# Second-layer attention by two passes: row maxima first, transposed exponentials after

## What is computed

```python
q = rope(x @ wq); k = rope(x @ wk); v = x @ wv       # 16 heads of 16; 4 key/value groups, each used by 4 heads
scores = einsum('bhqd,bhkd->bhqk', q, repeat(k)) / sqrt(16)
attn = softmax(where(causal, scores, -inf), axis=-1)
out = einsum('bhqk,bhkd->bhqd', attn, repeat(v)) @ wo
```

## Time and profile before

| | |
|---|---|
| median of 3 runs | 3948.26 us (3943.38 to 3952.19) |
| profiled execution, its own time | 3947.97 us |
| its span, first to last instruction | 3946.2 us |
| attention phase in it | about 2534 to 3281 us, of which the loop 2582 to 3271 |
| busy over the span | PE 3549.4, DVE 2593.0, ACT 2338.5, POOL 1374.7 us |

### The profile page before, as it was taken

The page is one execution under the profiler, slowest core; times in us unless marked ns, Lnnn a source line. Parts: engine busy times, 40 slices in busy tenths (PEclk is TensorE's granted clock), DMA queues, the critical chain, the costliest instruction groups (busy, mean ns, idle before and its releaser), DMA issues. The chain is left out here.

```text
span 3946.2 us, 76668 instructions
## 1 busy us (share of the span) xinstructions
PE 3549.4 (90%) x21286; PEld 2700.0 (68%) x21286; DVE 2593.0 (66%) x7383; ACT 2338.5 (59%) x5810; POOL 1374.7 (35%) x2264
## 2 busy tenths in 40 slices
PE   2999999999999999899999688788888886699996
PEld 2777777777777777678888544455656665588885
DVE  5777777777777777666666433356666664566665
ACT  2777777777777777655655411166666663255553
POOL 1333333333333333344343200144445440334442
PEclk9999999999999999999999778789999996799998
DMA  4222222222222222244343210100000003454554
GB/s 155 46 51 47 47 47 47 47 47 47 49 49 47 47 47 47 62 156 139 117 138 117 91 32 27 50 1 2 2 2 1 2 1 102 155 134 119 138 135 148
DMA packets 158496, 269.75 MB, mean 68 GB/s; under 512 B 19954, under 2 KB 106482, under 8 KB 158322
## 3 DMA queue, kind: packets, MB, share of 16 engines
q1 hardware_dynamic: 143730, 247.65, 21.5%
q0 software_dynamic: 14592, 19.93, 3.1%
HBM read 158.48 MB, written 40.89 MB: 51 GB/s over the span
## 5 line engine op out<-in xcount | busy, mean ns | idle before, releaser
L723 POOL TENSOR_SCALAR at_p<-at_p,at_recip 128x128 f32<-128x128 f32 (+3 forms) x1028 | 533.6, 532 | 982.8 <-DVE at_recip L862 982.8
L773 ACT ACTIVATE at_p<-at_p,at_nmax 128x128 f32<-128x128 f32 (+3 forms) x1030 | 575.8, 559 | 290.0 <-DVE at_nmax L856 286.8
L856 DVE CUSTOM_DVE_ANT_0 at_p<-at_s_ps,at_bias 128x128 f32<-128x128 f32 (+3 forms) x1030 | 492.5, 478 | 154.0 <-PE at_s_ps L971 154.0
L978 PE MATMUL at_t_ps<-ident,at_p 128*128 128x128 f32 x2560 | 459.8, 278 | 0.4 <-POOL at_p L723 0.4
L970 PE MATMUL at_s_ps<-at_k_twice,at_q 128*128 128x128 f32 (+3 forms) x1030 | 388.0, 377 | 7.9 <-DVE at_nmax L856 1.2
L1525 POOL TENSOR_SCALAR aa_p<-aa_p,aa_recip 128x128 f32<-128x128 f32 (+3 forms) x520 | 269.5, 537 | 329.4 <-DVE aa_recip L1667 329.4
L1552 ACT ACTIVATE aa_p<-aa_p,aa_nmax 128x384 f32<-128x384 f32 (+3 forms) x524 | 291.2, 558 | 149.6 <-DVE aa_nmax L1660 149.3
L1660 DVE CUSTOM_DVE_ANT_0 aa_p<-aa_s_ps,aa_hidden 128x384 f32<-128x384 f32 (+3 forms) x524 | 247.4, 484 | 135.4 <-PE aa_s_ps L1791 131.4
L971 PE MATMUL at_s_ps<-at_k_twice,at_q 128*128 128x128 f32 (+3 forms) x1030 | 332.5, 323 | 0.0
L978 PEld LDWEIGHTS at_t_ps<-ident,at_p 128*128 128x128 f32 x2560 | 294.6, 140 | 46.3 <-DVE at_pT L869 29.8
L988 PE MATMUL at_o_ps<-at_pT,at_v 128*64 128x512 f32 (+3 forms) x2064 | 306.3, 439 | 0.0
(11 more groups left out here) (307 smaller groups left out, 9070.2 us busy)
## 6 DMA issues: line engine op xcount, KB each, us to landing
at_k_twice<-at_k_parts SPq DMA_DIRECT2D x260, 256.0 KB, 3.3
nw_w_raw<-in_w_all_dram SPq DMA_DIRECT2D x52, 1024.0 KB, 7.4
w_raw<-in_w_dram SPq DMA_DIRECT2D x57, 768.0 KB, 5.9
ln_x<-in_x_dram SPq DMA_DIRECT2D x10, 512.0 KB, 5.0
nw_xh<-xh_dram SPq DMA_DIRECT2D x10, 512.0 KB, 4.3
nw_xl<-xl_dram SPq DMA_DIRECT2D x10, 512.0 KB, 4.9
rc_x<-x_dram SPq DMA_DIRECT2D x10, 512.0 KB, 3.8
at_w_raw<-in_w_heads_dram SPq DMA_DIRECT2D x18, 256.0 KB, 3.4
```

Source lines behind the costliest of these rows:

```text
L723: pool.tensor_scalar(p, p, recip[:, u:u + 1], 1.0, ALU.mult, ALU.mult).then_inc(scaled, 1)
L773: act.activation(p_sb[:, u, 0:N], p_sb[:, u, 0:N], ACT.Exp, bias=nmax[:, u:u + 1], scale=-1.0, accum_out=total[:, u:u + 1]).then_inc(exped, 1)
L856: dve.tensor_tensor_reduce(out=p_sb[:, u, 0:N], in0=s_ps[u % 2][:, 0:N], in1=bias[:, u % 2, S - N:S], scale=1.0, scalar=BIG, op0=ALU.add, ...
L978: ins = pe.transpose(t_ps[u % 2][:, k * P:k * P + P], p_sb[:, u, k * P:k * P + P], ident[:])
```

## The change

Each head is now handled in two passes. The first computes the scores as before, takes the row minimum and throws the scores away. The minimum, negated and split in a high and a low fp32r part, is transposed and placed by DMAs into two spare rows of the queries of its head, against two rows of ones in the keys. The second pass multiplies keys by queries, so that the product comes out transposed and with the maximum already subtracted; a small matmul (`late` by `once`) adds the causal mask of each diagonal block. ACT takes exp from PSUM into `pT` with no sum. v has columns of ones, so the value product also gives the sums of each row; it is done once a group of four heads over 512 columns. The sums are picked out (`add_up`), inverted on DVE, widened, multiplied back through the array (`spread_sums`) and applied in one DVE product (`norm`). POOL's scaling, PE's transposes of the exponentials and both engines' copies of them are gone. The samples' loop is written out; nothing is computed for a sample that does not exist. The first pass runs two groups ahead, and its mask writes back into its own PSUM bank.

```diff
-AHEAD = 3
-RING = 4
-QUADS = KV1 * TT
+STEPS1 = KV1 * REP
+PIECES = 3
+WIDTH = 2 * S + S // 2
...
-        s_ps = [ps(f"aa_s_ps{i}") for i in range(2)]
-        t_ps = [ps(f"aa_t_ps{i}") for i in range(2)]
-        o_ps = [ps(f"aa_o_ps{i}") for i in range(2)]
+        a_ps = [ps(f"aa_a_ps{i}") for i in range(2)]
+        b_ps = [ps(f"aa_b_ps{i}") for i in range(2)]
+        o_ps = ps("aa_o_ps")
+        w_ps = ps("aa_w_ps")
...
         @block.sync
+            for i in range(2):
+                for e in range(2):
+                    at = 64 * e + M_ROW
+                    for g in range(KV1):
+                        sp.dma_start(k_all[i][at:at + QD, e, g, :].bitcast(F32), ones).then_inc(ones_placed, 16)
+            for G in range(GROUPS):
+                n, g = divmod(G, KV1)
+                sp.wait_ge(act_out, out_by(PLACE[n, f"M{g}"]))
+                for h in range(REP):
+                    at = 64 * (h % 2) + M_ROW
+                    sp.dma_start(q_all[n % 2][at:at + 2, 2 * g + h // 2, :].bitcast(F32),
+                                 minusT[2 * h:2 * h + 2, :]).then_inc(placed, 16)
...
         @block.gpsimd
-            def scale(Q, q):
...
         @block.scalar
+            def exps(n, s, piece):
+                done = (n * STEPS1 + s) * PIECES + piece
+                N = S if piece < 2 else S // 2
...
+                act.wait_ge(pieced, done + 1)
+                act.activation(pT[group_of(n, s) % 2][:, s % REP, piece * S:piece * S + N], b_ps[done % 2][:, 0:N], ACT.Exp, scale=-1.0)\
+                    .then_inc(exped, 1)
...
+            for n in range(B):
+                for s in range(STEPS1):
+                    G = group_of(n, s)
+                    for piece in range(PIECES):
+                        exps(n, s, piece)
+                    if s % REP == 2 and G > 0:
+                        take_o(G - 1)
+                    if s == 0:
+                        take_minus(n, 1)
...
+                    if n + 1 < B:
+                        if s == 4:
+                            take_k(n + 1, 0)
+                            take_k(n + 1, 1)
+                        if s == 5:
+                            take_k(n + 1, 2)
+                            take_k(n + 1, 3)
+                        if s == 6:
+                            take_q(n + 1, 0)
+                            take_q(n + 1, 1)
...
         @block.vector
+            def mask(G, h, i):
...
+                dve.tensor_tensor_reduce(out=a_ps[i % 2][:, 0:N], in0=a_ps[i % 2][:, 0:N], in1=hidden[:, S - N:S], scale=1.0,
+                                         scalar=BIG, op0=ALU.add, op1=ALU.min, accum_out=nmax[:, G % 2, i, h:h + 1])\
+                    .then_inc(masked, 1)
...
+            def norm(G):
+                dve.wait_ge(spread_out, G + 1)
+                dve.tensor_tensor(oT[:, G % KV1, :], o_sb[:], w_ps[:], ALU.mult).then_inc(normed, 1)
...
+                    if h == 0 and G + 1 < GROUPS:
+                        part(G + 1)
+                    if G + 2 < GROUPS:
+                        for i in range(2):
+                            mask(G + 2, h, i)
+                    if h == 0 and G > 1:
+                        norm(G - 2)
+                    if h == 3 and G > 0:
+                        invert(G - 1)
+                    if G + 2 < GROUPS:
+                        for i in range(2, TT):
+                            mask(G + 2, h, i)
...
         @block.tensor
+            def score(G, h, i):
...
+                if done >= 2:
+                    pe.wait_ge(masked, done - 1)
+                pe.matmul(a_ps[i % 2][:, 0:N], q_all[n % 2][:, head // 2, N - P:N], k_all[n % 2][:, head % 2, g, 0:N],
+                          start=True, stop=True).then_inc(scored, 1)
+            def piece(n, s, part):
...
+                if h == 0 and part == 0:
+                    pe.wait_ge(placed, 16 * REP * (G + 1))
+                if done >= 2:
+                    pe.wait_ge(exped, done - 1)
+                for k, at in (((0, 0),), ((1, 0), (3, S - P)), ((2, 0),))[part]:
+                    pe.matmul(b_ps[done % 2][:, at:at + S - k * P], k_all[par][:, head % 2, g, k * P:k * P + P],
+                              q_all[par][:, head // 2, k * P:S], start=True, stop=False)
+                    ins = pe.matmul(b_ps[done % 2][:, at:at + P], late[:], once[:], start=False, stop=True)
+                ins.then_inc(pieced, 1)
...
+                for k in range(TT):
+                    for h in range(REP):
+                        ins = pe.matmul(o_ps[VP * h:VP * h + VP, k * P:S], v[n % 2][:, k, g, :],
+                                        pT[G % 2][:, h, BLOCK_AT[k]:BLOCK_AT[k] + S - k * P], start=(k == 0), stop=(k == TT - 1))
...
+            for G in range(2):
+                for h in range(REP):
+                    for i in range(TT):
+                        score(G, h, i)
+            turn_minus(0, 0)
+            for n in range(B):
+                more = n + 1 < B
+                for s in range(STEPS1):
+                    G, h = group_of(n, s), s % REP
+                    for part in range(PIECES):
+                        piece(n, s, part)
+                        if G + 2 < GROUPS:
+                            score(G + 2, h, part)
+                    if h == 1 and G > 0:
+                        weigh(G - 1)
+                    if G + 2 < GROUPS:
+                        score(G + 2, h, TT - 1)
+                    if h == 2 and G > 0:
+                        add_up(G - 1)
+                    if h == 3 and G > 0:
+                        spread_sums(G - 1)
+                    if s == 0:
+                        turn_minus(n, 1)
+                        if more:
+                            turn_x(n + 1)
+                    if s == 1 and more:
+                        project_kv(n + 1)
...
```

More of the change, by code:

```diff
@@ L1456, in attention_phase @@
[L1456 to L1470, removed]
+        GROUPS = B * KV1
+        FIRST = ["x0", "x1", "kk", "v", "q0", "s0", "q1", "s1", "k0", "k1", "k2", "k3", *(f"p{i}" for i in range(8)), "M0"]
@@ L1780, in score @@
-            def score(Q, q, par, h):
-                g, N = q // TT, (q % TT + 1) * P
-                head = g * REP + h
-                bank, at = s_place(q, h)
-                if h == 0:
-                    pe.wait_ge(masked, Q * REP + 2)
-                elif h >= 2:
-                    pe.wait_ge(masked, Q * REP + (h + 1))
-                pe.matmul(s_ps[bank][:, at:at + N], q_all[par][:, head // 2, N - P:N], k_all[par][:, head % 2, g, 0:N],
-                          start=True, stop=True).then_inc(scored, 1)
@@ new lines, in spread_q, with turn_minus @@
+            def spread_q(n, i):
+                bank_free(n, f"p{i}")
+                m, pair_of = divmod(i, 4)
+                pe.wait_ge(q_turned, 6 * n + 3 * m + 3)
+                pe.matmul(bank_of(n, f"p{i}")[:], spread[:, 0, pair_of, :], qh[:, m, :], start=True, stop=False)
+                pe.matmul(bank_of(n, f"p{i}")[:], spread[:, 1, pair_of, :], ql[:, m, :], start=False, stop=True)\
+                    .then_inc(made, 1)
+            def turn_minus(n, g):
+                bank_free(n, f"M{g}")
+                pe.wait_ge(parted, 2 * (n * KV1 + g) + 2)
+                for i in range(TT):
+                    ins = pe.transpose(bank_of(n, f"M{g}")[0:2 * REP, i * P:i * P + P],
+                                       minus[:, i].rearrange("p h c -> p (h c)").bitcast(F32), ident[:])
+                ins.then_inc(made, 1)
@@ new lines, in add_up, with spread_sums @@
+            def add_up(G):
+                pe.wait_ge(o_out, G + 1)
+                for i in range(TT):
+                    ins = pe.matmul(o_ps[:, i * REP:i * REP + REP], o_sb[:, i * P:i * P + P], pick[:], start=True, stop=True)
+                ins.then_inc(summed, 1)
+            def spread_sums(G):
+                pe.wait_ge(inverted, 2 * G + 2)
+                if G > 0:
+                    pe.wait_ge(normed, G)
+                for i in range(TT):
+                    ins = pe.matmul(w_ps[:, i * P:i * P + P], recip_wide[:, i].rearrange("p h d -> p (h d)"),
+                                    ident[:], start=True, stop=True)
+                ins.then_inc(spread_out, 1)
@@ L1881 @@
+            weigh(GROUPS - 1)
+            add_up(GROUPS - 1)
+            spread_sums(GROUPS - 1)
+            project_out(B - 1)
 E1 = 4
@@ L2590, in lay_out @@
         "spreads": spread_tables(),
+        "sums": sum_table(),
         "g2": by_partition(a["L1_ffn_g2"]),
```

627 lines of the change are left out of this document (309 added, 318 removed).

## The result

The changed kernel takes **3963.02 us** (median of 6 runs, 3959.24 to 3976.05), the kernel before on the same chip 3949.41 (3943.38 to 3953.56): ratio 1.0039, 95% interval 1.0022 to 1.0056. It is slower; the prediction had 3930 and put 0.28 on slower. The profiled execution took 3962.68 us.

The account below looks back on a forecast made before the run. Hand-overs between engines and loop turns were taken to bound the kernel. Gains of 25 us (turns) and 23 (unused work), less 17 of longer start, 6 of tail and the samples' difference: 3948 - 18 = 3930 us, range 3875 to 3990.

Parts of the forecast that it names:

- The gains: Attention loop: 25 us of loop turns and 23 us of work for samples that don't exist go away.
- The group by itself: Walk of four heads without projections: 2.87, 4.20, 3.86 and 3.75 us, sum 14.68 us a group.
- the second rival: Each head waits 0.15 us more than walked (mask into PSUM 0.1, semaphores): +19, a wash at 3949 us; chance 0.15.
- Part 3: Skill rule: weight loads overlap only across differing row groups; would add an estimated 100 us over 128 heads; given no chance.
- plus 8 for clock dips: Attention loop: 8 us added to 639.5 for dips of PE's clock, giving 648 us.
- the wait at `add_up`: Head 2 of each group: PE waits 0.68 us for ACT's `take_o`, queued behind three exps.
- 1.7 for ACT's eight 64-row copies of k: Steps 4 and 5 of a sample: exps queue behind these copies (0.585 us each), adding 1.7 us a sample.
- POOL's and DVE's other work ... nothing: Attention loop: the other work of these engines has half its time free, so it costs nothing.
- the walk: Step-by-step timing of heads through PE, masks and exps: 2.28 us a head, 83.4 us a full sample with projections.
- The third: Clock rival: PE stops and goes at every bank, notably steps 12 to 15, at 1.2 GHz: 3980 us; chance 0.28.
- a sample of over 88 us: Sign of a wrong forecast: clock below 0.9 means the clock rival, full clock means rings longer than walked.
- PE alone: First rival: waits in the heads are covered, PE's work alone decides; heads save 0.4 us each, 3880 us; chance 0.15.

Follow-up runs that it names:

- the kernel with `take_o` first: Changed kernel with ACT's take of the group's output moved ahead of that step's three exps: 3927.07 us, ratio 0.9946.
- The filled wait: Changed kernel with four more 128-column products, never read, ahead of each `add_up`, where PE waits for ACT's take of the output: 3942.75 us, ratio 0.9984.
- the kernel with all three edits: Changed kernel with `take_o` ahead of the exps, `part` behind its group's last mask, and k and q spreads dealt over the steps: 3908.14 us, ratio 0.9886.
- the even orders: Changed kernel, same work dealt over steps and placed between scores and pieces: 3884.93 us; then with M, `add_up` and `spread_sums` behind other work: 3856.68 us.

## Why the prediction was wrong

**Right.** The gains: 18 and 26 us for loop turns and unused work where 25 and 23 were put, 44 of 48. The start: first score at 2567.5 (2570), first piece at 2593.6 (2599.5); the scores took 20.6 us (24), and M 5.5 from its first transpose, as forecast. The group by itself: steps 12 to 14 take 2.5, 4.8 and 3.5 and step 15 3.4 at full clock, 14.1 against 14.68 (2.87, 4.20, 3.86 and 3.75, so that one head was put too short and three too long). Exp from PSUM 0.599 against the copy's 0.585; the mask in PSUM 0.09 us longer with its read, within its bounds, and without effect (3966 us with it in SBUF), so that the second rival's cause was not there; the M DMAs nothing after the first; no "issue" wait of microseconds. The rule of the Trainium skill, page "TensorE: Matmul & The Clock Gate", "Part 3", got no chance, and the trace bears that out for the most part: fp32 instructions of 256 columns start 0.22 us apart (32 output products in 7.07 us in the kernel with `take_o` first) and those of 512 columns 0.44, double, with nothing added for a load. In the pieces something of it may show: a 512-column product, its `late` product and the next start 0.32 and 0.06 us apart (at 3264.70, 3265.02 and 3265.08 in the changed kernel), 0.38 together where the 640 columns take 0.27 at 2.4 GHz and the prediction had 0.35.

**The step that failed** is "plus 8 for clock dips such as the earlier trace rows show". The lost clock is 46 us in 600; even the kernel before, with its turns written out, has 17. I had put the clock down as a small constant of the kernel before, and priced the wait at `add_up`, rightly placed, at its own length, 0.68 us. The wait is shorter than that (0.50 us in step 6, 0.43 in step 14, 0.23 in step 10), and taking it away is worth 36 us in 31 groups, 1.2 us each: some 0.35 of it wait, the rest clock in what comes behind. The filled wait shows the direction of cause: PE is held at that place for longer, but busy, and the kernel is 20 us faster.

**A second step was undersized**: "1.7 for ACT's eight 64-row copies of k". Dealing the spreads out gave 2.8 us a sample, and the lost clock falls by as much as the time, 20 us. Even dealt out, the twelve spreads take 9 to 10 us a sample and not 4.6 and 1.7, as the kernel with all three edits shows. ACT's sixteen copies of 0.6 us stand among the exps, and only the eight of k had a price; that these are the difference is likely but was not isolated. A third was put at nothing: `part` at 1.27 us instead of 0.18 beside POOL, 12 us; the prediction had "POOL's and DVE's other work ... nothing". With all three out of the way a sample is 82 to 85 us, where the walk had 83.4 (by luck in part, as said above), and the kernel takes 3908, below the forecast of 3930. What stays open is how the 55 us divide among the three: the first two draw on the same clock, the third on none of it by itself.

**The rivals.** The third had the sign and part of the mechanism, half clock in and around steps 12 to 15; but it blamed the stop and go at every bank. Steps 12 to 14 do stop and go at the rings, and run at full clock (2.51, 4.78, 3.46). Without the mask products PE waits more for exps (46.5 us against 20.1 from 2600 to 3160), and the lost clock is 43 us, no more than with them; with all of a step's work behind its last score, it waits 22.2 us for them and loses 1.7 of clock. The half clock goes when the stand at `add_up` goes, and in part when the spreads are dealt out. What the two have in common, by which the clock falls, no run here isolates; the length of a single stand is not it, since with `take_o` first PE stands up to 2.3 us for an exp and the clock is 0.97. So the rule of the Trainium skill that the prediction quoted for it, page "TensorE: Matmul & The Clock Gate", section "A second HAM failure mode: psum-queue depth-cycling", names a kind of idling that is there, but the trace does not bear out that the cycling of banks alone lowers the clock here. Of the prediction's signs, a sample of over 88 us came true, but at a clock of 0.92, between its two readings. PE alone (3880) is near what the even orders make of the kernel, 3885 and 3857; as the change was written, rings and stands were uncovered.

## What to carry to other kernels

Read the granted clock by windows beside the waits, and price a stand of PE by what runs at half speed behind it, not by its own length: here a wait of a quarter to a half of a microsecond, once a group, cost 1.2 us each time, and filling it with useless products paid. Before an exchange of passes is judged, split off what is not the exchange; here a written-out loop and dropped work gave the kernel before 44 us by themselves. Where rings of two banks are waited for, put the other work between their products and let the taking engines follow PE's order; that was worth more (106 us) than the change cost.

## What the runs showed of the hardware

- More work made the kernel faster: 124 products of 0.22 us, 3963.0 to 3942.8 us, at a clock of 0.98 instead of 0.92 from 2600 to 3200 us.
- PE was busy for all of the 10 us from 2810 to 2820 and its clock was 0.62; from 2900 to 2910, as busy, it was 0.51.
- The sum of PE's waits did not tell the clock: 45.4 us of them from 2600 to 3200 us went with a clock of 0.92, 45.8 with 0.97.
- A DVE mask that writes PSUM instead of SBUF takes 718 instead of 687 ns for 512 columns, and the read of its accumulator 140 instead of 82 ns.
- A DVE operation on 16 columns took 1.27 us instead of 0.18 beside a POOL addition in SBUF, and ended with it, in all seven cases.
- ACT's copies cost by their columns, not their rows: 8, 48 and 128 rows of 512 columns take 0.585, 0.591 and 0.596 us.
